# A fused condition + ternary feed-forward kernel: the seven block products of a pair of tiles in two PSUM banks, on top of copied partial sums, and the late condition products spread over three steps

## The reference, cut to what matters

```
cond = einsum('bnt,bot->bno', x, einsum('bg,got->bot', y, weight * mask)) + bias
bitlinear(x, w) = act_quant(x) @ weight_quant(w).T      # x to 127 steps of its row's maximum, w to -1, 0, 1
gate = silu(bitlinear(cond, w_gate)); up = bitlinear(cond, w_up)
out  = x + bitlinear(gate * up, w_down)
```

## Time and profile before

| | us |
|---|---|
| median of three runs | 464.94 |
| the profiled execution's own time | 464.25 |
| its span | 462.4 |
| PE busy | 444.5 (96%) |
| DVE busy | 338.7 (73%) |
| ACT busy | 288.7 (62%) |
| POOL busy | 156.8 (34%) |

### The profile page before, as it was taken

How to read it: one execution, slowest core, us unless ns; L and a number is a source line. 1 busy time by engine, 2 the same in 40 slices (tenths; PEclk the granted TensorE clock), 3 DMA queues, 4 the chain that set the end, 5 groups by cost and what they waited for, 6 DMA issues and landing times.

```text
span 462.4 us, 7082 instructions
## 1 busy us (share of the span) xinstructions
PE 444.5 (96%) x2184; PEld 236.2 (51%) x2222; DVE 338.7 (73%) x587; ACT 288.7 (62%) x381; POOL 156.8 (34%) x175
## 2 busy tenths in 40 slices
PE   4899999999999899999999999999999999999995
PEld 0234443444444355555555565565656555555562
DVE  0326779898956778787877878778787877878693
ACT  1216767775346767666676766667676676766660
POOL 0000251505291005342433524244352423524263
PEclk9999999999999999999999999999999999999999
DMA  8999996986212324554625345352544624245464
GB/s 283 404 403 412 411 234 154 378 229 146 48 35 43 71 47 102 128 117 107 127 63 136 85 105 132 87 136 45 136 105 105 139 61 136 68 114 127 102 138 136
DMA packets 104312, 69.77 MB, mean 151 GB/s; under 512 B 87264, under 2 KB 87264, under 8 KB 102752
## 3 DMA queue, kind: packets, MB, share of 16 engines
q1 hardware_dynamic: 103712, 67.39, 53.8%
q10 hardware_dynamic: 576, 2.10, 1.3%
HBM read 40.11 MB, written 8.39 MB: 105 GB/s over the span
## 4 chain that ended last, share of the span: by engine, by line
PE 73%; DMA 10%; SPq 6%; ACT 4%; DVE 3%; issue 3%; DVEq 0%; ACTq 0%
PE ps L690 46%; PE ps L709 19%; PE ps L659 8%; DMA wc<-w_gate 4%; DMA qT<-q_sb 3%; DMA wc<-w_down 2%; SPq L189 2%; SPq L182 1%; SPq L185 1%; ACT tern_up L353 1%; SPq L193 1%; ACT h_sb L359 1%; PE ps L717 1%; DMA wc<-wc 1%; ACT q_sb L364 1%
## 5 line engine op out<-in xcount | busy, mean ns | idle before, releaser
L375 ACT ACTIVATE wc<-ps,gate_unit 128x512 f32<-128x512 f32 x128 | 88.0, 689 | 97.6 <-PE ps L690 87.1
L570 DVE TENSOR_TENSOR wc<-ps,wc 128x512 f32<-128x512 f32 x128 | 88.4, 692 | 63.2 <-PE ps L690 46.0
L690 PE MATMUL ps<-tern_up,qT 128*128 128x512 bf16 x509 | 130.7, 379 | 0.2
L690 PE MATMUL ps<-tern_gate,qT 128*128 128x512 bf16 x477 | 126.1, 379 | 3.9 <-DVE wc L570 2.0
L659 PE MATMUL ps<-w_bot,xT_sb 128*128 128x512 f32 x256 | 113.2, 595 | 2.3 <-DVE w_bot L475 1.6
L690 PEld LDWEIGHTS ps<-tern_up,qT 128*128 (+1 forms) x512 | 50.1, 98 | 60.4
L575 DVE TENSOR_REDUCE p_part<-wc 128x1 f32<-128x1536 f32 x64 | 78.1, 1220 | 2.2
L659 PEld LDWEIGHTS ps<-w_bot,xT_sb 128*128 128x128 f32 x256 | 48.0, 190 | 61.3 <-issue 57.5
L690 PEld LDWEIGHTS ps<-tern_gate,qT 128*128 (+1 forms) x512 | 49.9, 98 | 44.6 <-issue 5.9
L389 ACT ACTIVATE wc<-wc 128x1024 f16<-128x1024 f32 x64 | 64.5, 1064 | 0.7 <-DVE wc L613 0.6
L709 PE MATMUL ps<-wc 128*128 128x256 f16 x480 | 62.2, 273 | 0.0
(11 more groups left out here) (63 smaller groups left out, 308.8 us busy)
## 6 DMA issues: line engine op xcount, KB each, us to landing
xT_sb<-xT SPq DMA_DIRECT2D x32, 256.0 KB, 6.8
x_res<-x SPq DMA_DIRECT2D x30, 256.0 KB, 2.8
out<-result SPq DMA_DIRECT2D x30, 256.0 KB, 2.2
wc<-wcond SPq DMA_DIRECT2D x12, 512.0 KB, 13.5
wc<-w_gate SPq DMA_DIRECT2D x4, 1024.0 KB, 17.3
wc<-w_up SPq DMA_DIRECT2D x4, 1024.0 KB, 12.2
wc<-w_down SPq DMA_DIRECT2D x4, 1024.0 KB, 7.6
wc<-wcond ACTq DMA_DIRECT2D x4, 512.0 KB, 7.6
```

The lines of the kernel that those rows point to most:

```text
L375: nc.scalar.activation(silu[:, c % 2], ps[:, GATE + c % 2], ACT.Silu, scale=unit).then_inc(silu_ready, 1)
L570: nc.vector.tensor_tensor(prod[:, par, 512 * c:512 * c + 512], ps[:, UP + c % 2], silu[:, c % 2], ALU.mult).then_inc(prod_ready, 1)
L690: ins = nc.tensor.matmul(ps[:, bank + c % 2], tile, w[:, c, k], start=(k == 0), stop=(k == KH - 1))
```

## The change

The seven products are taken in another order and gathered in two banks, `A` = 4 and `B` = 5. The new order is: `qsum0 x combo0` (A), `tile 2j half 0 x w` (A again, after the first was copied), `tile 2j half 1 x w` (B, on top of a copy of A), `qsum1 x combo1` (A), `qsum3 x w` (B, on top of A plus the first copy), `qsum2 x combo2` (A), `tile 2j+1 half 1 x combo3` (A). ACT copies A to SBUF (`copy_shared`) and from bank to bank (`copy_seed`), DVE writes a sum into bank B (`sum_seed`) and one out of A (`sum_c22`), ACT scales three finished blocks out of PSUM (`scale_c11`, `scale_c12`, `scale_c21`), POOL scales the fourth and adds the residual in two whole-tile adds (`finish_first`, `finish_second`). On ACT, POOL, DVE and SP the order within steps changes; the condition products of tiles 30 and 31 stand behind eight chunks of steps 0 to 2 in place of all eight of steps 0 and 1, and their `cond_tile` and `cond_round` move to steps 2 and 3. The plain product of tile 31 is cut in two around product 6.

```diff
-X, Z, V, LAST = 4, 5, 6, 7
+A, B, LAST = 4, 5, (6, 7)
+LATE_SLICES = {(0, 1): (0, 0), (0, 3): (0, 1), (1, 0): (0, 2), (1, 1): (0, 3), (1, 3): (1, 0), (2, 0): (1, 1),
+               (2, 1): (1, 2), (2, 2): (1, 3)}
...
             for s in range(1, TILES):
                 if s % 2 == 1 and s >= 5:
                     store(s - 5)
+                    store(s - 4)
                 transpose_q2(s - 1)
-                if s % 2 == 1 and s >= 5:
-                    store(s - 4)
...
+            def finish_first(j):
+                pool.wait_ge(c11_out, j + 1)
+                pool.wait_ge(c12_out, j + 1)
                 pool.wait_ge(s_xres[0], 16 * j + 16)
+                nc.gpsimd.tensor_tensor(result[:, 0], result[:, 0], x_res[:, 0], ALU.add).then_inc(result_ready, 1)
+
+            def scale_c22(j):
+                pool.wait_ge(c22_done, j + 1)
+                nc.gpsimd.tensor_scalar(result[:, 1, NB:HID], result[:, 1, NB:HID], out_unit[:, 2 * j + 1:2 * j + 2], 1.0,
+                                        ALU.mult, ALU.mult).then_inc(c22_scaled, 1)
+
+            def finish_second(j):
+                pool.wait_ge(c21_out, j + 1)
+                pool.wait_ge(c22_scaled, j + 1)
                 pool.wait_ge(s_xres[1], 16 * j + 16)
+                nc.gpsimd.tensor_tensor(result[:, 1], result[:, 1], x_res[:, 1], ALU.add).then_inc(result_ready, 1)
 
             for t in range(TILES):
+                if t >= 5 and t % 2 == 1:
+                    finish_second((t - 5) // 2)
+                elif t >= 4 and t % 2 == 0:
+                    finish_first((t - 4) // 2)
+                    scale_c22((t - 4) // 2)
                 unit_of(t)
...
+            def copy_seed(j):
+                act.wait_ge(down_psum, 7 * j + 2)
+                if j > 0:
+                    act.wait_ge(c12_out, j)
+                nc.scalar.activation(ps[:, B, 0:NB], ps[:, A, 0:NB], ACT.Copy).then_inc(seed_copied, 1)
...
+            def odd_step(s):
+                j = (s - 3) // 2 if s >= 3 else None
+                if s >= 5:
+                    scale_c21(j - 1)
                 silu_chunk(s, 0)
+                silu_chunk(s, 1)
+                round_tile(s - 1, 0)
+                if j is not None:
+                    copy_shared(j)
+                silu_chunk(s, 2)
+                convert(s - 1, 0, 0)
+                if j is not None:
+                    copy_seed(j)
+                silu_chunk(s, 3)
+                convert(s - 1, 0, 1)
+                if s == 3:
+                    cond_round(LATE + 1)
...
+            scale_c11(PAIRS - 1)
+            convert(TILES - 1, 1, 0)
+            scale_c12(PAIRS - 1)
+            convert(TILES - 1, 1, 1)
+            scale_c21(PAIRS - 1)
...
             def step(s, par, late=None, j=None, b0=0):
                 b1 = b0 + 1
+                if j is not None and par == 1:
+                    add_blocks(j, 0, b0, b1)
                 product(s, par, 0)
-                if j is not None and par == 1 and not (isinstance(j, int) and j == 0):
-                    join_blocks(j - 1)
                 if j is not None and par == 0:
+                    sum_seed(j)
                     add_blocks(j, 3, b0, b1)
                 product(s, par, 1)
                 if late is not None:
                     cond_tile(late)
                 if j is not None and par == 1:
-                    add_blocks(j, 0, b0, b1)
                     add_blocks(j, 1, b0, b1)
                 if j is not None and par == 0:
                     add_blocks(j, 2, b0, b1)
-                    finish_c11(j, s - 4)
                 product(s, par, 2)
+                if j is not None and par == 0:
+                    sum_c22(j)
                 largest(s, par, 0, 0, 3)
...
+                if i == 0 and not first:
+                    pe.wait_ge(c21_out, j)
+                if i == 1:
+                    pe.wait_ge(shared_copied, j + 1)
+                if i == 2:
+                    pe.wait_ge(seed_copied, j + 1)
+                if i == 4:
+                    pe.wait_ge(seed_summed, j + 1)
+                if i == 6:
+                    pe.wait_ge(c22_done, j + 1)
...
+                if i in (0, 3, 4, 5):
+                    pe.wait_ge(sum_ready, 4 * j + (1, 0, 0, 2, 3, 4)[i])
+                bank = (A, A, B, A, B, A, A)[i]
...
             down_product(PAIRS - 1, 3, b0, b0 + 1)
+            for half in range(2):
+                down_plain(LATE, half)
             down_product(PAIRS - 1, 4, b0, b0 + 1)
-            down_plain(LATE, LAST)
             down_product(PAIRS - 1, 5, b0, b0 + 1)
+            down_plain(LATE + 1, 0)
             down_product(PAIRS - 1, 6, b0, b0 + 1)
-            pe.wait_ge(c11_done, PAIRS)
-            down_plain(LATE + 1, X)
+            down_plain(LATE + 1, 1)
```

More of the change, by code:

```diff
@@ L390, in convert, with copy_shared @@
                                      ACT.Copy, bias=-ROUND).then_inc(q2_ready, 1)
[L392 to L401, removed]
-                silu_chunk(s, 0)
-                if even is not None:
-                    copy_part(even, 1)
+            def copy_shared(j):
+                act.wait_ge(down_psum, 7 * j + 1)
+                if j > 0:
+                    act.wait_ge(c22_done, j)
+                nc.scalar.activation(shared, ps[:, A, 0:NB], ACT.Copy).then_inc(shared_copied, 1)
@@ L405, in step, with even_step @@
+            def even_step(s):
+                j = (s - 4) // 2 if s >= 4 else None
+                if j is not None:
+                    scale_c11(j)
+                silu_chunk(s, 0)
                 silu_chunk(s, 1)
                 if s > 0:
[L407 to L411, removed]
+                    round_tile(s - 1, 1)
+                if j is not None:
+                    scale_c12(j)
@@ L412, in step @@
                 silu_chunk(s, 2)
-                if even is not None:
-                    copy_part(even, 3)
                 if s > 0:
                     for half in range(2):
-                        convert(s - 1, par, half)
-                if s in (1, 2):
-                    cond_round(LATE + s - 1)
+                        convert(s - 1, 1, half)
                 silu_chunk(s, 3)
+                if s == 2:
+                    cond_round(LATE)
             for i in range(4):
@@ L438, in _ @@
                     abs_sum_piece(*abs_after[t])
[L439 to L444, removed]
+            for s in range(0, TILES, 2):
+                even_step(s)
+                odd_step(s + 1)
+            scale_c11(PAIRS - 1)
[3 more added lines that the diff above has]
+            scale_c21(PAIRS - 1)
         @block.vector
@@ L531, in add_blocks @@
                         dve.wait_ge(s_q2T[half], 32 * j + 32)
-                    if not first:
-                        dve.wait_ge(down_psum, 7 * j)
+                if not first:
+                    dve.wait_ge(down_psum, 7 * j - (6, 3, 1, 2)[i])
                 if i in (1, 3):
@@ L538, in add_blocks, with sum_seed, sum_c22 @@
                 nc.vector.tensor_tensor(qsum[:, i], in0, in1, op).then_inc(sum_ready, 1)
-            def finish_c11(j, t):
+            def sum_seed(j):
+                dve.wait_ge(down_psum, 7 * j + 4)
+                dve.wait_ge(shared_copied, j + 1)
+                dve.wait_ge(c11_out, j + 1)
+                nc.vector.tensor_tensor(ps[:, B, 0:NB], ps[:, A, 0:NB], shared, ALU.add).then_inc(seed_summed, 1)
+            def sum_c22(j):
                 first = isinstance(j, int) and j == 0
-                dve.wait_ge(down_psum, 7 * j + 4)
-                dve.wait_ge(s_xres[0], 16 * j + 16)
+                dve.wait_ge(down_psum, 7 * j + 6)
                 if not first:
[L545 to L553, removed]
-                nc.vector.tensor_tensor(block_sum[:, 1], ps[:, Z, 0:NB], part[:, 0], ALU.add).then_inc(c21_done, 1)
-                dve.wait_ge(mid_done, 4 * j + 3)
-                nc.vector.tensor_tensor(block_sum[:, 0], ps[:, V, 0:NB], mid[:, 1], ALU.add).then_inc(c12_done, 1)
+                    dve.wait_ge(s_store[1], 16 * j)
+                nc.vector.tensor_tensor(result[:, 1, NB:HID], ps[:, A, 0:NB], shared, ALU.add).then_inc(c22_done, 1)
             def finish_last(i):
@@ L720, in _, with down_plain @@
+                ins.then_inc(down_psum, 1)
+            def down_plain(t, half):
+                pe.wait_ge(s_q2T[half], 16 * t + 16)
+                for k in range(KB * half, KB * half + KB):
+                    ins = nc.tensor.matmul(ps[:, LAST[t - LATE]], q2T[:, t % QBUF, k], tern_down[:, k], start=(k == 0),
+                                           stop=(k == KI - 1))
+                if half == 1:
+                    ins.then_inc(plain_psum, 1)
             pe.wait_ge(mix_w_ready, 3)
@@ L772, in step @@
                     if not odd:
-                        down_product(j, 3 + c, b0, b0 + 1)
+                        down_product(j, c + 3, b0, b0 + 1)
                     elif c > 0:
```

(2 more changed lines are left out.)

142 lines of the change are left out of this document (61 added, 81 removed).

## The result

| | before | changed |
|---|---|---|
| median of the runs, us (4 each) | 464.54 | 468.31 |
| range of the runs, us | 463.86 to 465.05 | 467.76 to 468.59 |
| the profiled execution's own time, us | 464.25 | 467.76 |
| its span, us | 462.4 | 466.0 |

The ratio is 1.0081, with a 95% interval of 1.0062 to 1.0099: the changed kernel is slower by 3.8 us.

A forecast was written before the change was run, and what follows sets the result against it. PE's issue of matmuls was taken as the bound, so only its waits count: start -0.5, steady steps +6.0, end +1.0 make +6.5 us, giving 470.75 or 471.4, stated as 471.0 us, range 465.0 to 474.0.

The forecast's parts named there:

- The steady steps: Odd steps 5 to 31: POOL's finish_second delays DVE's first sum, so product 0 waits 0.43 us, 14 times: +6.0 us.
- POOL's chain: In the odd step, tile unit at 199.65, 0.34 long, then finish_second from 200.07, holding POOL until 201.34.
- The rival on the other side: Odd steps: DVE's sum starts before POOL's add, the middle costs nothing, 464.75 or 465.4 us; chance 0.15.
- The start: Steps 2 and 3: cond_round behind the silu gains 0.9, sum_seed about 0.35 late for product 4; -0.5 us, bounds -2.0 and 0.
- The end: After step 31's start: last matmuls end 1.9 us later, earlier result stores give back 0.9; +1.0 us, bounds 0 and +2.2.
- the 14th wait: Last of the 14 odd-step waits of product 0, in step 31, 0.43 us; said to shift the whole end.
- The chain over `scale_c12`: At the end: product 4, scale_c12, tile 31's second convert, its transpose landing at 457.65, last 8 matmuls until 459.69.
- The covers: Other new waits (copy_shared, copy_seed, sum_seed, sum_c22) have time left; copy_seed ends 1 us before product 2.
- What it removes: Per pair, two ACT copies, three DVE operations and seven POOL instructions, against two whole-tile adds and one scaling; costed at nothing.

The follow-up runs named there:

- e1: Changed kernel with one more wait: POOL's finish_second waits until DVE has made the next pair's first sum; 463.03 us, ratio 0.9976 to the kernel before.
- e2: Changed kernel with POOL's finish_second cut into two adds of 128x256; 464.03 us, ratio 0.9995 to the kernel before.
- e6: Changed kernel with a 128x768 POOL add on scratch data ahead of finish_second in 14 odd steps; 475.16 us, ratio 1.0223 to the kernel before.
- e7: Changed kernel with the condition slices back behind all eight chunks of steps 0 and 1; 468.30 us, ratio 1.0075 to the kernel before.
- e4: Changed kernel with the first two condition slices behind chunks 0 and 1 of step 0, not 1 and 3; 466.37 us, ratio 1.0053.
- e3: Changed kernel with the last tile's second convert ahead of scale_c12 at the end of ACT's list; 467.21 us, ratio 1.0061 to the kernel before.
- e5: Changed kernel with the edits of e1, e3 and e4 together; 461.98 us, ratio 0.9950 to the kernel before.

## Why the prediction was right, and what was mis-sized

The direction, the mechanism and the place were right. I said 471.0 us, in a range of 465.0 to 474.0, and it is 468.31. The sum was 6.5 us, and the profiled executions differ by 3.5. All three terms came out lower than I had them, by 1.5, 0.8 and 0.9 us, so no error hid another.

- **The steady steps (+6.0; measured +4.5, as 4.23 in 13 steps and 0.3 in the last).** POOL's add does keep the sum out, in all 14 steps, and e1, e2 and e6 show it. `p_max` came at 1.11 us into the odd step, exactly as walked. What was mis-sized is POOL's chain behind it: I had let `finish_second` start 0.08 after the end of the unit, at 1.92; it started at 1.79, 0.31 after the unit's start, because POOL too begins its next instruction before the recorded end of the last one (199.12 against 198.81 + 0.34 = 199.15). The add then ended at 3.05 and not at 3.19, and the wait was 0.32 and not 0.43: 1.5 us over 14 steps. An odd step takes 9.81 to 9.87 us, where I had 9.95.
- **The rival on the other side** (the sum wins the race) was further off than its 0.15 says: the margin was 0.48 us or more and not 0.4, in every pair. The landings of 3.2 us that I counted on held.
- **The start (-0.5; measured -1.3).** Two terms were wrong. The wait of product 0 in step 3 was 0.34 and not 1.4 us. My walk had tile 1's first transpose at 155.3, 0.7 us ahead of step 3; the trace has it at 155.15, 1.6 us ahead, since step 3 starts at 156.74. I had counted the eight slices as three, three and two in steps 0, 1 and 2, where the table of the change has two, three and three; the later slices give tile 1's chain the time (e7 shows a wait of 1.14 without them). Steps 3 and 4 won 1.89 us in all. Against that, none of the two slices of step 0 stands behind chunk 0. ACT was still rounding the last condition tile and came to the first silu at 131.93, DVE's product followed, and chunk 2 met a bank that DVE had not left: 0.55 us (e4), a wait that I did not have at all.
- **The end (+1.0; measured +0.1).** PE's part was 1.48 us without the 14th wait (21.98 in e1 against 20.50), where I had 1.9: the transposes landed in 3.04 to 3.08, not 3.2, and the second half of tile 30 waited 0.45 and not 0.9. They were issued 2.6 us or more apart; in e3 and e5, where tile 31's two stand 1.3 us apart, they take 3.13 to 3.20. The stores at the very end won 1.37 us and not 0.9, since the last one is alone and lands in 2.00, where it took 2.53 before. The chain over `scale_c12` was right (e3).
- **The covers held.** The copies into and out of the banks and `sum_c22` never held PE up. Of the even steps only step 4 grew, by 0.09 us: its product 4 waited for a sum that came late behind the `units`. In "What it removes" I left out what comes in their place: three scalings of 0.47 us for each pair on ACT, and two adds on DVE. ACT is busy for 304.6 us and not 288.7, and that too cost nothing.

The rule of the Trainium skill in "SBUF — State Buffer" (Who interferes with whom), that the one that issues first keeps the other out for its whole instruction, holds here both ways round (1.29 and 1.66 us for DVE, 1.18 for POOL). The note of the Trainium skill in "Advanced Engine Details and Errata" (VectorE Performance Modes, Mode Summary), which names two-port instructions alone, would have left out, taken by itself, the effect that decides this change.

## What to carry to other kernels

An instruction on an idle engine is not free when it keeps out one that the critical engine waits for: what counts is whether it is running at the moment when the other is asked for, and how long that one instruction lasts. Before a sum is put closer to its deadline, list what POOL does in the microsecond before, and either order it behind the sum with a wait or cut it into pieces. And when work is moved on the bounding engine, walk each step with the new table in hand: where ACT or DVE is late, as in step 0, whether a chunk has a slice behind it decides if a later one meets its bank too early.

## What the runs showed of the hardware that was not expected

ACT's copy of 128x256 from PSUM takes 0.37 us whether it goes to SBUF or to another bank, but 0.46 to 0.48 with a scale that is read from a column. DVE's sum takes 0.43 us into PSUM, where the like one into SBUF took 0.41. DVE's product, which reads PSUM and one SBUF operand, is not held up by POOL: in e1, from 160 us on, 42 of them run beside an add of POOL and take 0.69 us as the other 73 do, and only the sum with two SBUF inputs is kept out. These rows are of the changed kernel, ACT and DVE:

```profile
197.53 0.48 ACT L408 ACTIVATE result<-ps,out_unit 128x256 f32<-128x256 f32 x1 [0.95 <-PE ps L740]
204.74 0.37 ACT L388 ACTIVATE ps<-ps 128x256 f32<-128x256 f32 x1
453.16 0.43 DVE L571 TENSOR_TENSOR ps<-ps,w_bot 128x256 f32<-128x256 f32 x1
```
